# The transposed, split context of two cross-attention layers kept in DRAM, in a Perceiver kernel on one Trainium2 core

## The reference, cut to what matters

```python
x = x + _L0_xattn_ref(_layernorm(x), ctx_1024, Wq, Wk, Wv, Wo, bo)            # 8 heads of 64
x = x + _L0_attn_ref(...); x = x + _L0_ffn_ref(...)
x = x + _L1_xattn_ref(_layernorm(x), ctx_1024, ctx_1024, wq, bq, wk, bk, ...)  # 16 heads of 16
x = x + _L1_attn_ref(...); x = x + _L1_ffn_ref(...)
# each cross-attention: k = ctx @ Wk, v = ctx @ Wv, out = softmax(q k^T / sqrt(d)) v, then Wo and bias
```

## Time and profile before

| | |
|---|---|
| median of 3 runs | 1873.9 us (1868.07 to 1879.59) |
| the profiled execution | 1879.48 us, span 1877.6 us |
| PE / DVE / ACT / POOL busy | 86% / 60% / 42% / 27% of the span |
| moved by DMA | 92.36 MB, mean 49 GB/s |

### The profile page before, as it was taken

One profiled execution on the slowest core, in us unless ns is written; L12 is line 12 of the kernel. 1 busy time (PEld: TensorE's weight loads), 2 busy tenths in 40 slices (PEclk: granted clock), 3 DMA queues, 4 the chain that ended last, 5 costly groups with the idle time before them and its releaser, 6 DMA issues. The chain is left out here.

```text
span 1877.6 us, 26948 instructions
## 1 busy us (share of the span) xinstructions
PE 1612.2 (86%) x10327; PEld 1203.1 (64%) x10327; DVE 1120.1 (60%) x1780; ACT 791.5 (42%) x1092; POOL 500.6 (27%) x630
## 2 busy tenths in 40 slices
PE   7989999999998678779997787998999899874298
PEld 6777777777776467568886564555665555332287
DVE  6866566666543565256664898777666776015641
ACT  4545545545442132224442224555555455652020
POOL 0023444434476000000000202444333444630000
PEclk9999999999999777579998998999999899997599
DMA  2122122222131100122230110110100100000253
GB/s 90 57 68 63 52 67 66 57 60 65 40 72 28 34 1 0 47 67 89 89 101 11 34 45 23 35 35 24 34 24 23 34 24 12 1 1 23 90 181 100
DMA packets 75445, 92.36 MB, mean 49 GB/s; under 512 B 7443, under 2 KB 62277, under 8 KB 75333
## 3 DMA queue, kind: packets, MB, share of 16 engines
q1 hardware_dynamic: 75140, 90.79, 16.4%
q10 hardware_dynamic: 192, 0.05, 0.0%
HBM read 73.47 MB, written 0.52 MB: 39 GB/s over the span
## 5 line engine op out<-in xcount | busy, mean ns | idle before, releaser
L596 POOL CAST st<-ef 32x512 fp32r<-32x512 f32 x384 | 233.5, 608 | 370.3 <-PE score L1214 327.5
L1788 DVE TENSOR_REDUCE mx<-bank 128x1 f32<-128x512 f32 x384 | 246.9, 685 | 97.0 <-PE bank L1229 96.4
L804 ACT ACTIVATE P<-score 128x1024 f32<-128x1024 f32 x256 | 251.3, 1023 | 125.0 <-PE score L1214 124.9
L1003 PE MATMUL bank<-c_hi,w_split 128*128 128x512 f32 x640 | 225.0, 410 | 24.8 <-DVE c_lo L1648 13.1
L1214 PE MATMUL score<-qs,st 97*128 97x512 f32 x512 | 174.3, 430 | 16.8 <-ACT P L804 11.5
L1229 PE MATMUL bank<-ef,qm 128*128 128x512 f32 x384 | 151.2, 445 | 30.1 <-DVE mx L1788 21.0
L1003 PEld LDWEIGHTS bank<-c_hi,w_split 128*128 128x128 f32 x640 | 123.6, 193 | 72.5 <-issue 18.6
L561 POOL TENSOR_TENSOR sum<-sum,P 128x512 f32<-128x512 f32 x84 | 111.2, 1324 | 210.0 <-ACT P L716 210.0
L716 ACT ACTIVATE P<-score 128x1024 f32<-128x1024 f32 x128 | 129.9, 1024 | 78.5 <-PE score L1039 76.1
L1003 PE MATMUL bank<-w_split,c_hi 128*128 128x256 f32 x768 | 147.5, 292 | 5.4 <-ACT v L814 5.4
L1229 PEld LDWEIGHTS bank<-ef,qm 128*128 128x128 f32 x384 | 73.2, 192 | 100.5 <-DVE mx L1788 80.4
(11 more groups left out here) (325 smaller groups left out, 2826.4 us busy)
## 6 DMA issues: line engine op xcount, KB each, us to landing
c_in<-in_ctx SPq DMA_DIRECT2D x64, 512.0 KB, 3.9
w<-k SPq DMA_DIRECT2D x128, 128.0 KB, 2.2
arena<-in_L_ffn_w SPq DMA_DIRECT2D x16, 1024.0 KB, 5.4
arena<-in_L_ffn_W SPq DMA_DIRECT2D x16, 1024.0 KB, 5.4
x<-in_x SPq DMA_DIRECT2D x1, 512.0 KB, 3.8
raw<-in_L_xattn_Wk SPq DMA_DIRECT2D x1, 512.0 KB, 6.7
raw<-in_L_xattn_Wq SPq DMA_DIRECT2D x1, 512.0 KB, 7.5
raw<-in_L_xattn_Wv SPq DMA_DIRECT2D x1, 512.0 KB, 8.3
```

The costliest lines, as they stand in the source:

```text
L596: pool.tensor_copy(st1[32 * block:32 * block + 32, k, :], ef1[rows, g % LAG, part, :].bitcast(F32)).then_inc(a[f"st{k}"], 16)
L804: act.activation(P1[:, index % PRING, :], score[n % 2][:], ACT.Exp).then_inc(a["p"], 1)
L1003: last = mm(dst, l, r, start=(n == 0), stop=(n == len(pairs) - 1))
L1788: v.tensor_reduce(mx1[:, u % 2, i, n:n + 1], bank_of(a, g + 1, f"m{n}")[:], AX.X, ALU.max).then_inc(a["red"], 1)
```

## The change

In the first layer, the chunks of units 0 and 2 are turned and split as before and then stored: `c_hi` and `c_lo` go to a DRAM tensor `split_ctx`, 512 KB each. In units 1 and 3 of the first layer, and in all four units of the second, the two parts are loaded from there, and no turn, copy, subtraction or load of the natural chunk is done. The first layer has one pair of buffers (`c0`) for both; the second has two pairs (`c1`), used in turn.

New semaphores: `cw` counts stores that have landed, `cr0` and `cr1` loads that have landed. In the first layer the load for chunk `t + 1` waits for the values matmuls of step `t`, and `keys` waits for the load; ACT waits for the store before it overwrites `c_hi`. In the second layer a load waits for the last matmuls that read its buffer two chunks before. The diff, cut (lines between @@ tell the place):

```diff
+TURNED = CHUNKS // 2
+def half_index(g):
+    u, i = divmod(g, NCH)
+    return NCH * (u // 2) + i
+def is_turned(g):
+    return 0 <= g < CHUNKS and g // NCH % 2 == 0
...
+        c1 = [(at("c_hi1", 38912, [2, CHUNK], F32R), at("c_lo1", 43008, [2, CHUNK], F32R)), (c_hi, c_lo)]
+        split_ctx = nc.dram_tensor("split_ctx", (B, NCH, 2, 128, 2 * CHUNK), F32).ap()
...
-        order1 = ["t0", "t1", *(f"m{n}" for n in range(16)), "k0", "v0", "v1"]
-        early1 = ["k0", "v0", "v1", "t0", "t1"]
+        order1 = [*(f"m{n}" for n in range(16)), "k0", "v0", "v1"]
...
@@ done0: the bank of a context tile is in use only where the chunk is turned @@
-            chunk = t + (kind == "t")
-            return ({"t": "cl", "k": "kl", "v": "v"}[kind], 2 * chunk + n + 1) if 0 <= chunk < CHUNKS else None
+            if kind == "t":
+                return ("cl", 2 * half_index(t + 1) + n + 1) if is_turned(t + 1) else None
+            return ({"k": "kl", "v": "v"}[kind], 2 * t + n + 1) if 0 <= t < CHUNKS else None
...
@@ SP, first layer @@
+                def store_split(g):
+                    u, i = divmod(g, NCH)
+                    sp.wait_ge(a["cl"], a.n("cl", 2 * half_index(g) + 2))
+                    for part in range(2):
+                        sp.dma_start(split_ctx[u // 2, i, part], c0[part][:].rearrange("p f n -> p (f n)").bitcast(F32)).then_inc(a["cw"], 16)
+                def load_split(g):
+                    u, i = divmod(g, NCH)
+                    sp.wait_ge(a["vp"], a.n("vp", 2 * g))
+                    sp.wait_ge(a["cw"], a.n("cw", 32 * turned_up_to(g)))
+                    for part in range(2):
+                        sp.dma_start(c0[part][:].rearrange("p f n -> p (f n)").bitcast(F32), split_ctx[u // 2, i, part]).then_inc(a[f"cr{g % 2}"], 16)
...
                 context(1)
+                store_split(0)
                 for t in range(STEPS):
                     g = t - LAG + 1
                     if 0 <= g < CHUNKS:
                         for h in range(HPU0):
                             stage_keys(g, h)
-                    if t + 2 < CHUNKS:
+                    if is_turned(t + 2):
                         context(t + 2)
+                    if is_turned(t + 1):
+                        store_split(t + 1)
+                    if t + 1 < CHUNKS and not is_turned(t + 1):
+                        load_split(t + 1)
...
@@ SP, second layer @@
+            def load_split1(g):
+                a, (u, i) = a1, divmod(g, NCH)
+                if g >= 2:
+                    before_u, before_i = divmod(g - 2, NCH)
+                    if before_u % 2 == 0:
+                        sp.wait_ge(a["vp"], a.n("vp", values1(before_u, before_i) + 2))
+                    else:
+                        sp.wait_ge(a["kp"], a.n("kp", g - 1))
+                for part in range(2):
+                    sp.dma_start(c1[g % 2][part][:].rearrange("p f n -> p (f n)").bitcast(F32), split_ctx[u // 2, i, part]).then_inc(a[f"cr{g % 2}"], 16)
...
-                sp.dma_start(c_in[:], ins["ctx_1024"][0, 0:CHUNK].rearrange("(k p) d -> p k d", p=128)).then_inc(a1["ctx"], 16)
+                sp.wait_ge(a0["cw"], a0.n("cw", 32 * TURNED))
+                load_split1(0)
...
+                stage_free(3)
                 for g in range(1, CHUNKS):
-                    context(g)
+                    load_split1(g)
...
@@ ACT, first layer @@
+                if f == 0 and is_turned(g - 1):
+                    act.wait_ge(a["cw"], a.n("cw", 32 * turned_up_to(g - 1)))
...
-                    if t + 1 < CHUNKS:
+                    if is_turned(t + 1):
                         for f in range(2):
-                            context_high(a, c_hi0, t, t + 1, f)
+                            context_high(t + 1, f)
...
@@ PE, first layer, keys; the second layer waits for cr alone @@
-                    if n == 0:
-                        pe.wait_ge(a["cl"], a.n("cl", 2 * g + 2))
+                    if n == 0 and is_turned(g):
+                        pe.wait_ge(a["cl"], a.n("cl", 2 * half_index(g) + 2))
+                    elif n == 0:
+                        pe.wait_ge(a[f"cr{g % 2}"], a.n(f"cr{g % 2}", 32 * (half_index(g) // 2) + 32))
...
-                    if t + 1 < CHUNKS:
-                        turn(a, t, t + 1, 0)
-                        turn(a, t, t + 1, 1)
+                    if is_turned(t + 1):
+                        turn(t + 1, 0)
+                        turn(t + 1, 1)
...
@@ PE, second layer, steady steps (the calls of the lead-in and of weights1 go too) @@
-                        if n in (1, 4) and t < CHUNKS:
-                            turn(a, t, t, n // 4)
...
@@ DVE, second layer, steady steps (likewise) @@
-                        if LAG <= t < CHUNKS and h in (2, 5):
-                            context_low(a, c_hi, c_lo, t, t, h // 4)
```

More of the change, by code:

```diff
@@ L44, in unit_of, with turned_up_to @@
     return divmod(u, 2)
+def half_index(g):
[3 more added lines that the diff above has]
+    return 0 <= g < CHUNKS and g // NCH % 2 == 0
+def turned_up_to(g):
+    return sum(is_turned(n) for n in range(g + 1))
 def perceiver(nc, ins, out):
@@ L96, in perceiver @@
         qh0 = at("qh0", 31744, [3, HPU0, S], F32R)
-        c_hi0, c_lo0 = (at(f"c_{part}0", 41984 + 1024 * n, [2, CHUNK], F32R) for n, part in enumerate(("hi", "lo")))
+        c_hi0, c_lo0 = c0 = [at(f"c_{part}0", 41984 + 1024 * n, [2, CHUNK], F32R) for n, part in enumerate(("hi", "lo"))]
         ql0 = at("ql0", 48128, [2, HPU0, S], F32R)
@@ L208, in done1 @@
             if kind == "m":
-                return ("red", 16 * (t - 1) + n + 1) if t <= CHUNKS else None
-            chunk = t + (kind == "t" and t < LAG)
-            if not 0 <= chunk < CHUNKS or (kind == "t" and t < LAG <= chunk):
+                return ("red", 16 * (t - 1) + n + 1) if LAG <= t <= CHUNKS else None
+            if not 0 <= t < CHUNKS:
                 return None
@@ L791, in weights1 @@
                         act.activation(hi[:, :, 0:256], pt.rearrange("p (f n) -> p f n", f=2), ACT.Copy).then_inc(set1["w0"], 1)
-                for f in range(2):
-                    context_high(a1, c_hi, -1, 0, f)
             def cross1():
@@ L846, in cross1 @@
                             values(u, i, 1)
-                        if t + 1 < LAG:
-                            for f in range(2):
-                                context_high(a, c_hi, t, t + 1, f)
                         if t == NCH:
@@ L1178, in weights1 @@
                     last.then_inc(set1["wT"], 1)
-                for f in range(2):
-                    turn(a1, -1, 0, f)
             def cross1():
@@ L1586, in _ @@
             pe.wait_ge(const_ready, 1)
-            turn(a0, -1, 0, 0)
-            turn(a0, -1, 0, 1)
+            turn(0, 0)
+            turn(0, 1)
             layer_norm(0)
@@ L1811, in cross1 @@
                     low_weights(set1, n, lo[:, :, 0:256], score[0][:, 512 * n:512 * n + 512].rearrange("p (f n) -> p f n", f=2), hi[:, :, 0:256])
-                for f in range(2):
-                    context_low(a, c_hi, c_lo, -1, 0, f)
                 dve.wait_ge(set1["bias"], 16 * 21)
@@ L1844, in cross1 @@
                         finish(g // NCH - 1)
-                    if t + 1 < LAG:
-                        for f in range(2):
-                            context_low(a, c_hi, c_lo, t, t + 1, f)
                     if i == 0 and 0 < t < CHUNKS:
```

67 lines of the change are left out of this document (29 added, 38 removed).

## The result

The changed kernel takes **1829.1 us** in the median of 4 runs (1825.23 to 1830.23), the kernel before 1874.95 beside it (1868.07 to 1879.59): ratio 0.9755, 95% interval 0.9727 to 0.9783. The forecast was 1820; the measured time lies at the upper edge of its inner range (1812 to 1829) and inside the wide one (1808 to 1839).

What follows compares the result with a forecast made beforehand. PE was taken to bound the first layer and DVE the second's lead-in, with PE waiting for reductions in its steady part. Savings of 18.5 and 35.4 us, 53.9 together, took the median 1873.9 to 1820 us (1812 to 1829; wide 1808 to 1839).

Steps and rivals of the forecast that it cites:

- First layer, steady steps: 14 steady first-layer steps without a turn at their end each gain 1.5 us on PE, 21 us in all.
- The load: First-layer load of both chunk halves takes 5.9 us, hidden behind 7.6 us of cover with 1.7 to spare.
- The store: Storing a turned chunk's halves takes 7.1 us, hidden within 7.85 us at its tightest, in the first layer's lead-in.
- The hand-over: At step 8 of the first layer, the first loaded chunk lacks cover: 2.5 us net loss, ends 1 and 6.
- Second layer, start and lead-in: Second layer before its steady steps: 2.65 us gained at the start, 7.5 in the lead-in where DVE sets the step.
- Second layer, steady: 23 steady second-layer steps gain 1.1 us each, as reductions run without the first subtraction and transposes: 25.3 us.
- (a): Rival: second layer gains only 0.7 us a step, exponentials or banks becoming the wait; 1833 us; chance 0.18 with (e).
- (e): Rival: other users hold the maxima's banks equally late, so only PE time goes; 1839 us; chance 0.18 with (a).
- (b): Rival: DVE and PE savings add up in the second layer, 1.5 us a step; 1811 us; chance 0.09.
- (d): Rival: first-layer keys wait for loads, 14 us per microsecond beyond cover; chance 0.04 as no change, 0.03 as slower.
- (c): Rival: traffic only partly hidden, loads at 8.3 us and stores in sequence; 1850 us; chance 0.06.

Runs made afterwards that it cites:

- early8_div: `early8` with DVE's division at the first layer's unit ends moved ahead of the step's low keys; 1815.8 us, ratio 0.9681 to the kernel before.
- first_only: Changed kernel, but the second layer loads natural chunks and turns them all as before; 1862.7 us, ratio 0.9935 to the kernel before.
- no_loads: Changed kernel without the split-context loads, except the first layer's first and the second layer's first two (wrong context); 1827.8 us.
- dve_kept: Changed kernel with two DVE operations on a spare buffer at the old subtraction places in 23 steady second-layer steps; 1851.7 us.
- after_again: The changed kernel unedited, measured again beside `early8` and `early8_div`; 1828.6 us, ratio 0.9758 to the kernel before.
- pe_kept: Changed kernel with 2 x 4 PE transposes of a constant kept at the old places in 23 steady second-layer steps; 1837.5 us.
- early8: Changed kernel with chunk 8 loaded early into its own buffer and chunk 9's load one step earlier; 1822.1 us, again 1821.3.
- dve_first: Changed kernel with one DVE reduction put back at the first subtraction's place in 23 steady second-layer steps; 1846.8 us.
- traffic2: Changed kernel with two 512 KB DRAM-to-DRAM copies issued ahead of each first-layer load; 1900.6 us, kernel before there 1871.0.
- second_only: Changed kernel, but the first layer turns all its chunks and only the second loads split ones; 1839.1 us, ratio 0.9812 to the kernel before.
- traffic4: Changed kernel with four 512 KB DRAM-to-DRAM copies issued ahead of each first-layer load; 1950.8 us, kernel before there 1871.0.

## Why the prediction was right, and where not

The direction and the mechanism held; the time came 9 us above the forecast, at the edge of its inner range. By its own steps:

**First layer, steady steps (21 us)**: a loaded step lost 1.5 us, 17.05 to 15.47 or 15.57, as said, by the 0.80 of the turns and the stall of the first maxima. Not as said is the count of 14 clean steps. Where unit 3 begins, steps 25 to 27 give 2.2 us instead of 4.5, each for a reason of its own. In step 25 PE waits 0.78 us for ACT's copies of the values where the turns had been, in step 26 there was no stall of the maxima, so that only the turns' 0.80 went, and in step 27 DVE's division sets the time in both kernels: from the reciprocal's start to the next reduction it is 6.64 us before and 6.12 after, though 1.29 us of subtraction left, because the low queries between them take 1.48 us instead of 0.80. Both run beside a sum on POOL (404.46 to 405.98 us in the changed kernel); where POOL is idle, as at this place in `early8_div`, they take 0.41. The prediction asked "what is late next" of an ordinary step only. `early8_div` bears the third reason out: with the division moved, step 27 is 15.47 long. All steps with less work (10 to 16 and 24 to 32, by their first exponentials) lost 18.6 us where 21 were forecast, and 2.3 of the missing 2.4 are these three. Another 1.5 went in step 19, whose code is unchanged: 20.57 us instead of 19.05, at a granted clock of 0.91 instead of 1.00 (see the last section). With the 4.0 of the hand-over that leaves 13.1. The last 2.2 of the layer's 15.3 came behind the last chunk's exponentials (27.4 us instead of 29.6, mean granted clock 0.88 instead of 0.83), and they are no gain of the change: `first_only`, `no_loads` and `dve_kept`, with the changed kernel's code there, take 29.4 us at 0.83.

**The load (5.9 us of 7.6 cover)**: in the first layer's steady steps the second half lands 5.1 us after its issue in the median and is issued some 0.4 us behind the first, 5.5 us in all (over both layers its median is 4.2); at the hand-over it is 5.98 us from the first issue to the keys. The cover was right too: 8.05 us less 0.49 of wait in the late step are 7.56. But the price is not the same each time, which the prediction left out. In the changed kernel one of the 15 steady loads comes late, in `after_again` one by 0.88 us (8.4 us from first issue to landing), in `pe_kept` one by 0.90, in `early8_div` one by 0.45; in `first_only`, `early8` and `dve_first` none. So it is hidden nearly always and not by 1.7 us for certain. The 8.2 us that the prediction estimated from the Trainium skill (DMA: Bandwidth & Descriptors) are not the rule here, 5.5 us is; but single loads reach them. The page's row for 1 MB is of transfers issued from GpSimd, these are issued by SP.

**The store (7.1 of 7.85)**: hidden. Its halves land in 3.5 and 4.6 us, no copy of ACT waits for it, and the first layer's lead-in steps are as long as before (10.16 to 10.45 us before, 10.19 to 10.43 after).

**The hand-over (2.5 us net, ends 1 and 6)**: 4.0 (first exponentials 119.5 against 115.5 us), within the ends, short by 1.5. The wait was sized rightly (3.78 us, keys 2.6 us later than before); what was too small was the clock: PE runs most of keys(8) at the slower level, and behind the wait for the row maximum all of the values, of which it was about half before. Over the 14 us from the keys on the granted clock is 0.62 (102 to 116 us), before it was 0.88 (99 to 113). From the keys' start to the matmul behind the row maximum it is 10.03 us instead of 8.58, and from there to the exponentials 7.36 instead of 7.46, so that the turns' 1.5 us were hardly gained. `early8` puts the whole of it at 5 to 7 us.

**Second layer, start and lead-in (10.15)**: 12.3 (10.9 to 12.3 over the runs with this code there). The start was under-sized: keys(0) come 10.4 us after the stage's start instead of 13.5, 3.1 us sooner where 1.3 were forecast, and the queries' chain follows after 5.9 instead of 8.1, 2.3 where 1.35 were forecast. The lead-in itself gave the remaining 6.9 (forecast 7.5).

**Second layer, steady (25.3)**: 20.8. Sixteen ordinary steps lost 1.06 each, 16.9 us, as said (1.1). The seven around unit boundaries, with divisions, shifts and sums, lost 3.8 us instead of 7.7; steps 11, 19 and 26 among them nothing (0.1, -0.35 and 0.0). That is largely the clock and not the change: these three take 16.87, 23.41 and 16.29 us at granted clocks of 0.90, 0.85 and 0.90, and in `early8`, alike there, 16.00, 22.57 and 15.53 us at 1.00, 0.92 and 1.00, nearly the clocks that they had before (1.00, 0.93 and 1.00). By `early8` and `no_loads` the 23 steps lost 23.3 and 23.6 us, 2 less than forecast. Behind the 23 steps another 1.0 us went the other way, which makes the layer's 32.0. The split of the 1.1 was right: the first subtraction counts in full (0.67 a step in `dve_first`), the second not at all (`dve_kept`), as forecast, and PE's transposes add 0.5 on their own, more than the 1.1 leaves for them (0.4).

**Rivals.** (a), 0.7 a step in the second layer, falls: the ordinary steps lost 1.06. (e), that the banks stay held, falls: the first pair of maxima takes 0.47 us as it should, and `dve_first` shows DVE's share. (b), that savings add up to 1.5, falls: parts of 0.67 and 0.5 make 1.2 singly, and 1.1 together. (d) is right in kind and hardly in force (0.49 us in one step); its price was too low. With loads late by 3.3 us the prediction's 14 us for each would be 46, measured were 72. So its point of decision comes sooner: `traffic2`, with 3.3 us of wait in each of 16 loaded steps, is already 1.6% slower than before (1900.6 against 1871.0, one run each), at 11.2 us from first issue to keys, where the prediction had said 12.8. (c), partly hidden traffic, falls: the stores are hidden and the loads nearly always.

In sum 18.5 + 35.4 were predicted and 15.3 + 32.0 found. What was mis-sized is the hand-over's clock (1.5 us) and the steps where a unit begins, which were costed by an ordinary one (2.3 in the first layer). The rest is mostly the clock: 1.5 us in step 19 of the first layer, some 2.5 in three steps of the second, and 2.2 in the other direction behind the first layer's loop. By luck these and the start of the second layer, which gave 2.7 more than forecast, nearly cancel.

## What to carry over

Cost a change of a pipelined loop at its boundaries too, not only at its ordinary step: there another wait can stand right behind what leaves, and take up the gain. Look for such waits even where the change does not touch them: the division (3.35 us behind the low keys) made PE wait before the change as well, and it belongs ahead of the wait in which its engine idles. Compare a load with its cover by its slowest instance, not only by its median (5.5 and 8.0 us here, against 7.6). Where a recomputation is replaced by a load, first look for the one place where the load has no cover, and give it a buffer of its own. A microsecond by which the loads were late cost here 1.2 to 1.4.

## What was not expected of the hardware

A wait of PE costs more than itself. After 3.3 us of wait in each loaded step, the mean granted clock of these steps was 0.92 instead of 1.00 (`traffic2`), and the layer lost 72.3 us for 52.8 of waits. Around 2.06 us of wait at the unit boundary it was 0.68 for 4 us. Which of the two levels (1.2 and 2.4 GHz) PE gets is not wholly a matter of the program. Step 19 of the first layer, a turned step with the same code in all these kernels but `early8_div`, takes one of two lengths: 19.05 to 19.07 us in five of them (before, `second_only`, `pe_kept`, `traffic2`, `traffic4`) and 20.56 to 20.58 in the others. Its windows, in the kernel before and in the changed one, show it in the clock; PE's waits are the same in both (one of 1.52 and one of 1.53 us):

```profile
270.00:289.00 19.00, 17.34 (x118) 13.60 (x118) 13.02 (x21) 9.42 (x15) 7.72 (x6) 1.00 0.23 58
```

```profile
266.00:285.00 19.00, 18.53 (x117) 14.97 (x117) 11.65 (x19) 8.11 (x13) 7.57 (x6) 0.91 0.31 105
```

Step 27 does the same: 19.94 us in the kernel before and 18.43 in `second_only`, behind waits of 1.52 and 1.53 us, with granted clocks of 0.57 and 1.00 in the four microseconds behind. In `early8_div`, where these waits are gone, the clock stays at 1.00 in both places. So a wait of 1.5 us can be followed by the slower level or not; what decides it no run here shows, and a single step's length can be off by 1.5 us.

A DVE operation can be longer beside POOL. The first operation of `dve_kept`, with both inputs in SBUF, took 0.88 to 1.13 us in 20 of 23 steps beside POOL's casts, and 0.68 where POOL was idle; the reduction at the same place in `dve_first`, with one input, 0.67 to 0.69 us in all 23. The low queries of the first layer went the same way (0.41, 0.80 and 1.48 us).
